# The first feed-forward product of a cross-attention block by Strassen's scheme, in blocks of 1024 tokens

## The reference

```python
xq  = layer_norm(x, qn_w, qn_b);  ctx = layer_norm(context, cn_w, cn_b)
q, k, v = heads(xq @ q_w), *heads(ctx @ kv_w)
attn = softmax(where(mask, -FLT_MAX, q k^T * scale))
x = x + (attn v) @ proj_w + proj_b
h = layer_norm(x, n2_w, n2_b)
h = gelu(h @ fc1_w + fc1_b) @ fc2_w + fc2_b      # exact GELU; fc1_w 512 x 2048, fc2_w 2048 x 512
return x + h
```

## Time and profile before

| | |
|---|---|
| median of 3 runs | 1123.36 us |
| the profiled execution's own time | 1124.4 us |
| its span, first to last instruction | 1122.6 us |
| busy: TensorE, VectorE, ScalarE, POOL | 1106.7, 572.7, 403.5, 233.6 us |
| mean granted TensorE clock, as a share of 2.4 GHz | 0.998 |
| moved by DMA | 48.76 MB |

### The profile page before, as it was taken

How to read it: one execution, slowest core, us unless ns; L and a number is a source line. 1 busy time by engine, 2 the same in 40 slices (tenths; PEclk the granted TensorE clock), 3 DMA queues, 4 the chain that set the end, 5 groups by cost and what they waited for, 6 DMA issues and landing times.

```text
span 1122.6 us, 16405 instructions
## 1 busy us (share of the span) xinstructions
PE 1106.7 (99%) x5857; PEld 941.0 (84%) x5857; DVE 572.7 (51%) x1153; ACT 403.5 (36%) x1162; POOL 233.6 (21%) x187
## 2 busy tenths in 40 slices
PE   8999999999999999999999999999999999999998
PEld 6799999999999788888888888888888888888887
DVE  7888888878897755533332423322322332332212
ACT  4566556655666544311311211311221221121110
POOL 3334543455445501101100100100110110010000
PEclk9999999999999999999999999999999999999999
DMA  7011121141110143210001002002002001000101
GB/s 249 15 48 38 42 72 38 38 122 60 56 40 20 53 136 113 57 52 24 1 11 66 1 2 75 1 1 75 1 1 76 1 1 40 36 1 1 38 1 38
DMA packets 40193, 48.76 MB, mean 43 GB/s; under 512 B 11014, under 2 KB 19246, under 8 KB 40136
## 3 DMA queue, kind: packets, MB, share of 16 engines
q1 hardware_dynamic: 39551, 46.89, 12.7%
q10 hardware_dynamic: 584, 1.06, 0.3%
HBM read 30.54 MB, written 16.78 MB: 42 GB/s over the span
## 4 chain that ended last, share of the span: by engine, by line
PE 82%; DVE 13%; ACT 2%; issue 2%; DMA 1%; DVEq 0%; ACTq 0%
PE bank L1420 31%; PE bank L1391 31%; PE bank L1290 8%; PE bank L1248 4%; PE bank L1229 3%; DVE nmax L890 2%; DVE PTl L913 2%; DVE bnst L937 2%; DVE xTl L896 1%; PE bank L1403 1%; DVE xhat L949 1%; DVE S L883 1%; DVE qTl L902 1%; DVE aTl L918 1%; PE bank L1279 1%
## 5 line engine op out<-in xcount | busy, mean ns | idle before, releaser
L1420 PE MATMUL bank<-w,gTh 128*128 128x512 f32 x1024 | 319.2, 393 | 0.0
L1130 DVE CAST gTh<-g 128x512 fp32r<-128x512 f32 x128 | 56.9, 445 | 443.0 <-ACT g L795 443.0
L795 ACT ACTIVATE g<-bank,cols 128x512 f32<-128x512 f32 x128 | 88.2, 689 | 471.2 <-PE bank L1391 470.0
L1420 PEld LDWEIGHTS bank<-w,gTh 128*128 128x128 f32 x1024 | 192.4, 188 | 42.7
L1420 PE MATMUL bank<-w,gTl 128*128 128x512 f32 x512 | 200.4, 391 | 0.0
L1391 PE MATMUL bank<-hT0h,w 128*128 128x512 f32 x512 | 162.2, 398 | 0.4 <-DVE w L1087 0.4
L1391 PE MATMUL bank<-hT1h,w 128*128 128x512 f32 x512 | 159.2, 392 | 0.1
L487 POOL TENSOR_TENSOR hrs<-hve,mhalf 128x1 f32<-128x1 f32 x32 | 17.6, 550 | 551.5 <-DVE hve L1104 551.5
L1420 PEld LDWEIGHTS bank<-w,gTl 128*128 128x128 f32 x512 | 96.1, 188 | 22.0
L1391 PEld LDWEIGHTS bank<-hT0h,w 128*128 128x128 f32 x512 | 94.7, 188 | 22.2 <-DVE w L1087 0.6
L1391 PEld LDWEIGHTS bank<-hT1h,w 128*128 128x128 f32 x512 | 95.1, 188 | 20.0 <-issue 0.8
(11 more groups left out here) (108 smaller groups left out, 1790.7 us busy)
## 6 DMA issues: line engine op xcount, KB each, us to landing
xr<-in_x SPq DMA_DIRECT2D x16, 512.0 KB, 3.4
x_scratch<-xr SPq DMA_DIRECT2D x16, 512.0 KB, 2.8
x<-x_scratch SPq DMA_DIRECT2D x8, 1024.0 KB, 5.7
out<-x SPq DMA_DIRECT2D x7, 1024.0 KB, 4.3
w1raw<-in_L_xattn_fc_w SPq DMA_DIRECT2D x16, 256.0 KB, 3.0
w2raw<-in_L_xattn_fc_w SPq DMA_DIRECT2D x16, 256.0 KB, 2.8
kvw<-in_L_xattn_kv_w ACTq DMA_DIRECT2D x1, 1024.0 KB, 9.8
qraw<-in_L_xattn_q_w SPq DMA_DIRECT2D x4, 256.0 KB, 7.6
```

Source lines behind the costliest of these rows:

```text
L795: act.activation(g[:, :], bF[j % 2][:, :], ACT.Gelu, bias=cols[:, F1B + j:F1B + j + 1]).then_inc(a_gelu.sem, 1)
L1130: dve.tensor_copy(gT[HI][j % 4][:, :], g[:, :]).then_inc(v_ghi.sem, 1)
L1420: mm = pe.matmul(bC[t][:, :], gT[d][j % 4][:, t * P:(t + 1) * P], w2[:, j, w, :], start=(j == 0 and i == 0), stop=(j == JT - 1 and i == 2))
```

## The change

The first product h @ fc1_w is taken per block of 1024 tokens (4 blocks) and per set s of 256 hidden columns (8 sets: slices s and s+8). The 512 x 256 weights and the 512 x 1024 tokens are split in quarters: weights A11..A22 of 256 x 128, tokens B11..B22 of 256 x 512. In place of eight products of quarters there are seven, M1 to M7, of combinations of them; each is 2 k-tiles x 3 products = 6 matmuls. The four quarters of the result are sums of the products.

- Weight side: POOL forms four sums per set (`w1_sums`), ScalarE and VectorE split the seven combinations (`w1_hi`, `w1_lo`, four instructions each). This is done once, in block 0, where the sets are stored to DRAM; later blocks load each set again (1.8 MB, `load_w1`), and likewise the second weights (1.0 MB a set, `load_w2`), whose remainder is now POOL's (`w2_lo`).
- Token side: per block POOL forms four sums T1 to T4 of the normalised quarters (`hop_T`); ScalarE makes seven HI operands of 1024 numbers a partition (`hop_hi`), VectorE four of the remainders and POOL three (`hop_lo`).
- Result side: VectorE builds the four quarters with seven adds, each from a PSUM bank (`y_add`); ScalarE takes the GELU of each and makes its HI, VectorE its LO (`g_lo`).
- Second product: no longer accumulated in PSUM over all slices. After each set eight token tiles of 6 matmuls go through two PSUM banks in turn, and VectorE adds each into an accumulator in SBUF (`acc_add`); POOL adds the bias there first (`acc_bias`). `fc2` of tile t waits for the add of tile t-2.
- Norm: eight tiles of a block instead of four. Those of block 0 are normalised in units 6 to 13, those of the next block in sets 1 to 5 (`TILES`).
- Units 13 to 15 (`tail` 0, 1, 2) hold the first set's weight sums, the first block's operands, and M1, M2 (unit 14) and M5, M6 (unit 15).

The diff, cut to its core (buffers, semaphores and most waits for free buffers left out).

Constants: order of the products, sums and tiles.

```diff
+    TILES = {1: (0, 1), 2: (2,), 3: (3, 4), 4: (5,), 5: (6, 7)}
...
+    GROUPS = ((slice(C_A11, C_A22), w1raw[:, 0, :, :]), (slice(C_A22, 7), w1raw[:, 1, 1:2, :]),
+              (slice(C_S1, C_A11), sums[:, C_S1:C_A11, :]), (slice(0, C_S1), sums[:, 0:C_S1, :]))
...
+    HOPS = (B11, B21, T1[:, :, :], T2[:, :, :], T3, B22, T4[:, :, :])
+    HOP_T = (None, None, 0, 2, 1, None, 3)
+    ON_POOL = (4, 5, 6)
+    M1, M2, M5, M6, M7, M3, M4 = range(7)
+    MULS = ((C_A11, bank[0]), (C_A12, bank[1]), (C_S1, bank[2]), (C_S2, bank[3]), (C_S3, bank[5]), (C_S4, bank[0]),
+            (C_A22, bank[1]))
...
+    ADDS = ((0, M2, 1), (1, M6, 1), (2, M7, 1), (1, M5, 1), (3, M5, 2), (1, M3, 1), (2, M4, 2))
+    GS = ((0, C11, 0, FIRST), (3, C22, 1, SECOND), (1, C12, 0, SECOND), (2, C21, 1, FIRST))
...
```

SP, the streamed weights:

```diff
+        def load_w1(block, s):
+            t_M.wait(sp, block, 7 * (s - 2) + 6)
+            sp.dma_start(f32(w1r[:, w1_slot(s), :, :, :]).rearrange("p c d n -> p (c d n)"), w1_scr[s]).then_inc(
+                d_w1[w1_slot(s)], 16)
+        def load_w2(block, s):
+            t_fc2.wait(sp, block, BT * (s - 1) - 1)
+            sp.dma_start(f32(w2r[:, s % 2, :, :, :]).rearrange("p j d n -> p (j d n)"), w2_scr[s]).then_inc(d_w2[s % 2], 16)
...
```

POOL, units 13 to 15 and a block:

```diff
+            if tail == 0:
+                w1_sums(0)
+            if tail == 1:
+                hop_T(0, (0, 1, 2))
...
+            if tail == 1:
+                hop_T(0, (3,))
+            if tail == 2:
+                hop_lo(0, 4)
+                hop_lo(0, 5)
+                w1_sums(1)
+                hop_lo(0, 6)
...
+        def h_rstd(b, t):
+            v_hve.wait(pool, b, t)
             power(hrs[:, :], hve[:, :], P).then_inc(p_hrs.sem, 1)
...
+        def hop_lo(b, i):
+            a_hop.wait(pool, b, i)
+            pool.tensor_tensor(hop[i][:, LO, :, :], HOPS[i], f32(hop[i][:, HI, :, :]),
+                               ALU.subtract).then_inc(p_hop.sem, 1)
+        def w2_lo(s):
+            a_w2.wait(pool, 0, s)
+            pool.tensor_tensor(w2r[:, s % 2, :, LO, :], w2raw[:, :, :], f32(w2r[:, s % 2, :, HI, :]),
+                               ALU.subtract).then_inc(p_w2.sem, 1)
...
+        def block(b, before, first=False, last=False):
+            for s in range(SETS):
+                if first and 0 < s < SETS - 1:
+                    w1_sums(s + 1)
+                if first:
+                    w2_lo(s)
+                if s == 0:
+                    if first:
+                        pool.wait_ge(d_fc2b, 16)
+                    for t in range(BT):
+                        acc_bias(b, t)
+                if not last:
+                    for t in TILES.get(s, ()):
+                        h_rstd(b + 1, t)
+                    if s == SETS - 2:
+                        hop_T(b + 1, range(4))
+                    if s == SETS - 1:
+                        for i in ON_POOL:
+                            hop_lo(b + 1, i)
...
```

ScalarE, units 14 and 15 (first halves) and a block:

```diff
+            if tail == 1:
+                hop_hi(0, 0)
+                w1_hi(0, 0)
+            if tail == 2:
+                m1_copy(0, 0)
+                hop_hi(0, 3)
+                w1_hi(0, 3)
...
+        def gelu(b, s, i):
+            n, add, half, v = GS[i]
+            y = ybuf[n]
+            v_c.wait(act, b, 7 * s + add)
+            j = s + half * SETS
+            act.activation(y[:, :], y[:, :], ACT.Gelu, bias=cols[:, F1B + j:F1B + j + 1]).then_inc(a_gelu.sem, 1)
+            if i == 0:
+                t_fc2.wait(act, b, BT * (s - 1) - 1)
+            a_gelu.wait(act, b, 4 * s + i)
+            act.activation(gT[s % 2][:, half, HI, v], y[:, :], ACT.Copy).then_inc(a_ghi.sem, 1)
...
+        def block(b, before, first=False, last=False):
+            for s in range(SETS):
+                refill = not last and s == SETS - 1
+                if first and s == 0:
+                    t_proj.wait(act, last_unit, UT - 1)
+                else:
+                    m1_copy(b, s)
+                gelu(b, s, 0)
+                if refill:
+                    hop_hi(b + 1, 0)
+                gelu(b, s, 1)
+                if refill:
+                    hop_hi(b + 1, 1)
+                gelu(b, s, 2)
+                gelu(b, s, 3)
+                if refill:
+                    for i in range(2, 7):
+                        hop_hi(b + 1, i)
+                if first and s + 1 < SETS:
+                    for i in range(4):
+                        w1_hi(s + 1, i)
                 if first:
-                    w2_hi(j)
-                if first and j + W1_AHEAD < JT:
-                    w1_hi(j + W1_AHEAD)
-                if not last and j - 1 in NORMS:
-                    h_hi(s.plus(1), NORMS.index(j - 1))
-
-        blocks(act, step2)
+                    w2_hi(s)
+                if not last:
+                    for t in TILES.get(s, ()):
+                        h_raw(b + 1, t)
...
```

VectorE, units 14 and 15 and a block (`add(s, t)` is `acc_add` of set s-1, or of the last set of the block before):

```diff
+            if tail == 1:
+                hop_lo(0, 0)
+                w1_lo(0, 0)
+            if tail == 2:
+                y_add(0, 0, C11)
+                hop_lo(0, 3)
+                w1_lo(0, 3)
...
+            if tail == 1:
+                hop_lo(0, 1)
+                w1_lo(0, 1)
+                w1_lo(0, 2)
+                hop_lo(0, 2)
...
+        def h_normed(b, t):
+            p_hrs.wait(dve, b, t)
+            dve.tensor_scalar(hring[t % 2][:, :], hring[t % 2][:, :], hmv[:, 0:1], hrs[:, 0:1], ALU.subtract,
                               ALU.mult).then_inc(v_hhat.sem, 1)
+        def y_add(b, s, i):
+            n, m, other = ADDS[i]
+            t_M.wait(dve, b, 7 * s + m)
+            if i == C11:
+                a_cp.wait(dve, b, s)
+            if i in (U3, C22, C12):
+                v_c.wait(dve, b, 7 * s + (U2, U3, U4)[(U3, C22, C12).index(i)])
+            if isinstance(b, int) and b == 0 and s == 0 and i == C22:
+                dve.wait_ge(d_x2st, 16 * NU)
+            dve.tensor_tensor(ybuf[n][:, :], MULS[m][1][:, :], ybuf[other][:, :], ALU.add).then_inc(v_c.sem, 1)
...
+        def acc_add(b, s, t):
+            t_fc2.wait(dve, b, BT * s + t)
+            if s == 0:
+                p_acc.wait(dve, b, t)
+            dve.tensor_tensor(acc[t][:, :], bY[t % 2][:, :], acc[t][:, :], ALU.add).then_inc(v_acc.sem, 1)
...
+            for s in range(SETS):
+                refill = not last and s == SETS - 1
+                tiles = () if last else TILES.get(s, ())
+                if not (first and s == 0):
+                    y_add(b, s, C11)
+                g_lo(b, s, 0)
+                y_add(b, s, U2)
+                y_add(b, s, U3)
+                y_add(b, s, U4)
+                y_add(b, s, C22)
+                y_add(b, s, C12)
+                y_add(b, s, C21)
+                add(s, 0)
+                if refill:
+                    hop_lo(b + 1, 0)
+                if len(tiles) > 0:
+                    h_stats(b + 1, tiles[0])
+                    v_hbn.wait(dve, b + 1, tiles[0])
+                g_lo(b, s, 1)
+                if len(tiles) > 0:
+                    h_variance(b + 1, tiles[0])
+                add(s, 1)
+                g_lo(b, s, 2)
+                g_lo(b, s, 3)
+                if len(tiles) > 0:
+                    h_normed(b + 1, tiles[0])
+                if refill:
+                    hop_lo(b + 1, 1)
+                if first and s + 1 < SETS:
+                    w1_lo(s + 1, 0)
+                    w1_lo(s + 1, 1)
+                add(s, 2)
+                if len(tiles) > 1:
+                    h_stats(b + 1, tiles[1])
+                    v_hbn.wait(dve, b + 1, tiles[1])
+                add(s, 3)
+                if len(tiles) > 1:
+                    h_variance(b + 1, tiles[1])
+                if refill:
+                    hop_lo(b + 1, 2)
+                if first and s + 1 < SETS:
+                    w1_lo(s + 1, 2)
+                    w1_lo(s + 1, 3)
+                add(s, 4)
+                if len(tiles) > 1:
+                    h_normed(b + 1, tiles[1])
+                add(s, 5)
+                if refill:
+                    hop_lo(b + 1, 3)
+                add(s, 6)
+                add(s, 7)
...
```

TensorE, units 14 and 15 and a block (`out(s, t)` is `fc2` of set s-1):

```diff
+            if tail == 2:
+                mul(0, 0, 2, first=True)
...
+            if tail == 1:
+                mul(0, 0, 0, first=True)
...
+                h_T(0, norm2)
+            if tail == 1:
+                mul(0, 0, 1, first=True)
+            if tail == 2:
+                mul(0, 0, 3, first=True)
...
+        def mul(b, s, i, first=False):
+            c, bank_ = MULS[i]
+            for kk in range(2):
+                for n, (w, d) in enumerate(PRODUCTS):
+                    mm = pe.matmul(bank_[:, :], w1r[:, w1_slot(s), c, w, kk * P:(kk + 1) * P], hop[i][:, d, kk, :],
+                                   start=(kk == 0 and n == 0), stop=(kk == 1 and n == 2))
+            mm.then_inc(t_M.sem, 1)
...
+        def fc2(b, s, t, first=False):
+            if t == 0:
+                v_glo.wait(pe, b, 4 * s + 3)
+                if s < SETS - 1:
```

(24 more changed lines are left out.)

656 lines of the change are left out of this document (364 added, 292 removed).

## The result

The changed kernel takes 1178.7 us (median of 4 runs, 1177.6 to 1179.7) against 1123.7 before (1122.2 to 1124.2): a ratio of 1.049 [1.047, 1.051], slower. The forecast was 1165 us, range 1120 to 1200. The profiled execution took 1177.6 us, span 1175.8.

The account below looks back on a forecast made before the run. TensorE was taken to bound the kernel, busy 99% of the span. From 1124.4 us, -43.5 + 1 + 17 + 46 + 12 + 1 + 8 = +41.5 gave 1166, as median of runs 1165 us; range 1120 to 1200.

Parts of the forecast that it names:

- the prediction's signs: Expected observations: block 0 near 215 us, middle and last blocks near 175, five TensorE gaps of about 5 us in block 0.
- Units up to 13; units 14 and 15: Attention units: +1 us for four tiles normalised earlier; +12 (5 to 20) for operand and weight work in units 14, 15.
- Blocks 1 and 2: Middle blocks: normalising, refill and POOL's sums delay adds to the output, 8.5 us a block, +17 together (8 to 30).
- POOL's power behind the second weights' remainder: Block 0: power ends near 19.1 us into a set, delaying scaling, add of f2 and f4; block 0 +46 in all.
- Rival 4: Block 0: POOL's power not last; weight remainders alone delay adds, 3 us a set; 1141 us, chance 0.07.
- The clock: Behind seven longer TensorE gaps the granted clock falls, costing 1.7 us each, partly hidden in five: +8 (0 to 12).
- Rival 2: Block 0: clock stays low, matmuls at half rate whenever VectorE is not last; +22 to 1187 us, chance 0.15.
- Streamed weights at nothing: Weight loads, 2.9 MB a set, need 15.7 us of a 20.4 us set, issued one to two sets ahead: no cost.
- rival 3: The stream binds: 31.9 us a set, +10 in 24 sets, 1400 us, chance 0.05; sign: TensorE gaps ending with a DMA.
- POOL beside VectorE: Remainders meeting POOL's operand sums in set 6: only the first slowed, 0.4 us a middle block; 9 more possible by lock rule.
- What goes: Feed-forward stage: seven quarter products instead of eight remove 192 of 3072 matmuls at 0.227 us, -43.5 us.
- Rival 1: Adds to the output never late, the 32 sets losing under 1 us each on average: 1103 us, chance 0.12.

Follow-up runs that it names:

- experiment 1: Changed kernel with, in block 0, POOL's power for a set's first tile ahead of the second weights' remainder: 1156.7 us, 1.030 of the kernel before.
- experiment 3: Changed kernel with sixteen unused extra products where TensorE stands, in sets 1 to 5 of block 0: 1165.9 us, 1.038 of the kernel before.
- experiment 5: Changed kernel, SP queue in set 0 of blocks 1 to 3: weight load behind stores and reloads, two x tile loads ahead (blocks 1, 2): 1169.5 us, 1.042.
- experiment 8: Experiment 7's kernel with POOL's remainder of the second weights moved to the next set's start in block 0: 1116.7 us, 0.994 of the kernel before.
- experiment 7: Changed kernel reordered throughout: SP's queue, last units and set 0, POOL's powers earlier, VectorE's adds of f0 to f2 as in ordinary sets: 1125.8 us, 1.002.
- experiment 9: Experiment 8's kernel with further reordering of POOL's bias adds and sums, SP's loads, unit 15's remainders and set 7's copies: 1102.6 us, 0.982.

## Why the prediction was right

The time lies inside the range and the mechanism is the one forecast, but the sum hides two errors that partly cancel: the losses came out 25 us larger than forecast and the gain 13.6 us larger. That the total is only 12 us off is luck in part. Blocks 0 to 3 took 210, 180, 181 and 181 us where the prediction's signs had 215, 175, 175 and 175. In the table a loss is what a set takes over 90 matmuls at 0.227 us and 0.36 us a normalised tile; for the units it is the difference to the kernel before.

| Term | Predicted, us | Measured, us |
|---|---|---|
| Units up to 13; units 14 and 15 | 1; 12 | 2.6; 15.3 |
| Block 0, sets 0 and 1 | 16.8 | 19.9 |
| Block 0, sets 2 to 5, with the clock | 26 + most of 8 | 32.1 |
| Block 0, sets 6 and 7 | 3.3 | 8.4 |
| Blocks 1 and 2 | 17 | 28.9 |
| Last block | 1 | 3.1 |
| Sum | 85 | 110 |

- **POOL's power behind the second weights' remainder** was right in place and time (18.6 measured, 19.1 placed), and experiment 1 shows its worth, 22 us, the clock behind the stalls included. Rival 4, by which the power isn't last, fell.
- **The clock** (8): the right size as far as block 0 tells, 8.0 in sets 1 to 5 (experiment 3), but not as it was divided. There 1.0 was placed in each of the five sets; the fall cost 2.8 in sets 2 and 4, 1.2 in sets 3 and 5, and nothing in set 1. What it cost in the units and in set 0 wasn't tested. The price itself was read from a longer stall than stated: around TensorE stood from 10.26 to 12.23, 2.0 us and not 1. Rival 2 fell: after the transposes of set 2 the clock was 0.66, but block 0 as a whole got 0.89, and its sets 2 to 6 start at 1.00 (set 1 at 0.50, set 7 at 0.65 in their first microsecond).
- **Streamed weights at nothing** failed. Bytes were the wrong measure: rival 3 fell, since experiment 5 streams as much, but order in SP's queue cost 9.2 us. No step of the prediction looked at what else the 1.8 MB load delays. Its sign for rival 3, waits of TensorE that go back to a DMA, came although rival 3 is false.
- **Blocks 1 and 2** (17): sets 2 to 5 lost 1.2 to 1.4 each, as placed (1.15). The difference lies in set 1 (2.9 and 6.0, SP's queue) and in the refilling set 7 (4.9 and 3.3 instead of 2.2), which no run changed alone.
- **POOL beside VectorE** was sized too small. One meeting a block was counted, and one in unit 14; set 6 of block 0 lost 5.8 instead of 1.1, unit 14 had two such remainders (2.8 and 3.2 us), and 9 us lay in it once the other waits were gone (experiment 8). In blocks 1 and 2 set 6 took 20.6, so that there the sums cost nothing: the count depends on the order of both engines in each set. The Trainium skill (SBUF — State Buffer, "Who interferes with whom") says that the pair of ports is locked for a whole instruction; the 5.07 in set 6 of block 0 agrees. The same section of the Trainium skill says that a VectorE instruction with at most one SBUF input is spared unless it runs in a mode that uses both port pairs, which `tensor_scalar`, the instruction of the scaling, can under conditions. The adds from PSUM agree, 0.6 us beside POOL in experiment 1; the 2.49 of a scaling in experiment 7 would fit the exception, but no run here shows in which mode it ran.
- **What goes** (-43.5) was too small. With 110 of losses it would give 1124.4 + 66.8 = 1191. The difference to 1177.6, 13.6, was in the kernel before: its 3048 feed-forward matmuls (3072 less the units' 24) at 0.227 and 28 transposed tiles at 0.36 make 702 of the 714.2 us. So by this yardstick it had 12 us of losses itself, not as waits but in matmuls that started 0.231 us apart on the mean, and losses counted from zero leave these out; four fewer tiles in this stage give 1.4.
- **Rival 1**, adds never late, was put at 1103 with losses under 1 us a set: experiment 9 comes to 1102.6. It wasn't what this order does, but what the scheme allows. That the two numbers meet is luck: counted as in the table, experiment 9 still loses some 36 us where the rival had 22, and the 13.6 of the point above make up for it.

Not settled: in experiment 9 the units still end some 10 us later than before the change, with unit 14 in part at a lower clock, and sets 0 and 1 of block 0 lose another 10; in blocks 1 and 2 half a microsecond a set remains.

## What to carry to other kernels

When work is taken off the bounding engine by giving more to others, place one period instruction by instruction in every queue, DMA queues included, and put what the bounding engine waits for ahead of what it doesn't; busy shares (69% for VectorE here) say nothing of it. Put POOL's long instructions beside VectorE's PSUM reads, not beside its SBUF work (experiment 8). And measure the losses of the old schedule by the same yardstick as those of the new.
